# Probability transposes in chunks of 128 keys, and x2 moved to a multiple of 256 bytes, in a fused decoder layer

## The reference

```python
q = _split_heads(queries @ W_q + b_q)          # 16 heads of 32
k = _split_heads(keys @ W_k + b_k)
v = _split_heads(values @ W_v + b_v)
scores = jnp.einsum('bhqd,bhkd->bhqk', q, k) / jnp.sqrt(jnp.float32(d))
scores = jnp.where(mask == 0, jnp.float32(-1000000.0), scores)
attn = jax.nn.softmax(scores, axis=-1)
out = jnp.einsum('bhqk,bhkd->bhqd', attn, v)
...
return out @ W_o + b_o
...
x = _layernorm(x + _L0_ffn_ref(x, ...), axis=-1)   # x @ (kernel) + bias + (x @ a) @ b
```

## Time and profile before

| | |
|---|---|
| median of 3 runs | 945.8 us (941.78 to 947.99) |
| profiled execution | 944.69 us, its span 942.9 us |
| TensorE busy | 892.1 us, 4,348 matmuls |
| VectorE busy | 674.7 us |
| ScalarE, GpSimd busy | 377.3 us, 376.6 us |
| mean granted clock of TensorE | 0.981 |

### The profile page before, as it was taken

One profiled execution on the slowest core, in us unless ns is written; L12 is line 12 of the kernel. 1 busy time (PEld: TensorE's weight loads), 2 busy tenths in 40 slices (PEclk: granted clock), 3 DMA queues, 4 the chain that ended last, 5 costly groups with the idle time before them and its releaser, 6 DMA issues.

```text
span 942.9 us, 14474 instructions
## 1 busy us (share of the span) xinstructions
PE 892.1 (95%) x4348; PEld 739.6 (78%) x4348; DVE 674.7 (72%) x1132; ACT 377.3 (40%) x1403; POOL 376.6 (40%) x338
## 2 busy tenths in 40 slices
PE   5798999999999999999689999999999999999997
PEld 4683888888888888888568788888888888888775
DVE  3364566666665757667578878889788897888957
ACT  4161221202121111001596466665656656566611
POOL 2000464435354343333236534335343453434723
PEclk9897999999999999999799999999999999999999
DMA  6961811331404020204503040321303214031021
GB/s 183 284 201 57 173 39 53 82 91 44 134 11 122 22 67 23 67 38 140 175 16 109 21 135 15 93 71 26 133 13 91 71 28 131 13 91 23 14 78 46
DMA packets 85211, 76.03 MB, mean 81 GB/s; under 512 B 39143, under 2 KB 57831, under 8 KB 85167
## 3 DMA queue, kind: packets, MB, share of 16 engines
q1 hardware_dynamic: 85167, 75.49, 27.1%
HBM read 52.60 MB, written 22.87 MB: 80 GB/s over the span
## 4 chain that ended last, share of the span: by engine, by line
PE 42%; DVE 4%; ACT 2%; issue 2%; POOL 2%; POOLq 0%; DVEq 0%
PE shared_ps L114 31%; PE score_ps L114 4%; PE shared_ps L1185 4%; ACT probs L1391 1%; PE shared_ps L1148 1%; PE shared_ps L1218 1%; POOL probs L1540 1%; DVE score_ps L1697 1%; DVE xT_lo L1654 1%; DVE x_and_res L1743 0%; DVE pT_lo L1681 0%; DVE top_s L1702 0%; POOL x_and_res L1555 0%; DVE y L1721 0%; DVE w_o_lo L1864 0%
## 5 line engine op out<-in xcount | busy, mean ns | idle before, releaser
L1391 ACT ACTIVATE probs<-score_ps,top_s 128x77 f32<-128x77 f32 x512 | 159.1, 359 | 36.8 <-DVE top_s L1702 36.8
L1391 ACT ACTIVATION_READ_ACCUMULATOR probs<-score_ps,top_s 128x1 f32 x512 | 122.9, 240 | 0.0
L1540 POOL TENSOR_TENSOR probs<-probs,per_total 128x616 f32<-128x616 f32 x64 | 82.7, 1309 | 64.7 <-DVE per_total L1709 64.5
L1533 POOL TENSOR_TENSOR rstd<-ve,half_power 128x1 f32<-128x1 f32 x64 | 42.4, 662 | 156.7 <-DVE ve L1732 152.2
L1697 DVE COPY_PREDICATED score_ps<-hidden,masked 128x616 f32<-128x616 int32 x64 | 67.2, 1050 | 9.4 <-PE score_ps L114 9.3
L97 POOL TENSOR_TENSOR xT_lo<-x_tok,xT_hi 128x512 fp32r<-128x512 f32 x28 | 39.0, 1394 | 85.6 <-ACT xT_hi L93 85.6
L1398 ACT ACTIVATE pT_hi<-shared_ps 103x512 fp32r<-103x512 f32 (+1 forms) x96 | 54.9, 614 | 45.1 <-PE shared_ps L1185 44.6
L713 ACT ACTIVATE qT_hi<-vals 128x512 fp32r<-128x512 f32 x32 | 19.3, 628 | 119.2 <-POOL vals L760 103.9
L760 POOL TENSOR_TENSOR vals<-qs_prod 128x512 f32<-128x512 f32 x32 | 41.0, 1293 | 62.7 <-DVE qs_prod L846 62.7
L1681 DVE TENSOR_TENSOR pT_lo<-shared_ps,pT_hi 103x512 fp32r<-103x512 f32 (+1 forms) x96 | 64.5, 684 | 0.0
L706 ACT ACTIVATE v_sb<-v_ps 128x512 f32<-128x512 f32 x32 | 18.9, 594 | 106.9 <-PE v_ps L114 106.9
(11 more groups left out here) (210 smaller groups left out, 2642.5 us busy)
## 6 DMA issues: line engine op xcount, KB each, us to landing
x_tok<-in_x SPq DMA_DIRECT2D x32, 256.0 KB, 4.6
x_res<-in_x SPq DMA_DIRECT2D x8, 1024.0 KB, 7.3
x_between<-mix_x SPq DMA_DIRECT2D x32, 256.0 KB, 2.0
x<-x_between SPq DMA_DIRECT2D x8, 1024.0 KB, 5.6
x_tok<-x_between SPq DMA_DIRECT2D x8, 1024.0 KB, 5.7
out<-y_out SPq DMA_DIRECT2D x32, 256.0 KB, 2.0
wqkv_sb<-in_w_qkv SPq DMA_DIRECT2D x16, 192.0 KB, 5.0
keys_split<-w_q_hi SPq DMA_DIRECT2D x8, 154.0 KB, 5.0
```

The costliest lines, as they stand in the source:

```text
L1391: nc.scalar.activation(probs[:, t % 2, j * KEYS:(j + 1) * KEYS], score_ps[:, g, k * KEYS:(k + 1) * KEYS], ACT.Exp, bias=top[:, t % 2, j:j ...
L1533: nc.gpsimd.tensor_tensor(rstd[:, n:n + 1], ve[:, n:n + 1], half_power[:], ALU.pow).then_inc(rstd_ready, 1)
L1540: nc.gpsimd.tensor_tensor(p, p, per_total[:, t % 2, h * heads:(h + 1) * heads].unsqueeze(2) .to_broadcast([P, heads, KEYS]), ALU.mult).the ...
```

## The change

`KC` is gone. The probabilities of a tile are now cut per half (616 columns: two groups) into four chunks of 128 keys and a tail of 104 (`TAIL`). Bank uses: c = 0 has the four wide chunks of half 0, c = 1 those of half 1, c = 2 the two tails. The use with c = 0 waits for the first half of the normalization, c = 1 for the second. A group's 308 keys lie in three chunks, of which the middle one of a half is shared with the other group (`group_chunks`); its rows of the other group are zeros in `v_block`. The value pieces are cut anew and now differ between even and odd groups (`v_pieces`), so each DMA carries two groups and there are twelve pieces instead of six. `pT` has 10 chunks instead of 12, which moves the tiles behind it by 8,192 bytes. `x2T` starts at column 1,280 of its tile instead of 1,248.

```diff
--- before.py
+++ after.py
@@ -34,7 +34,10 @@
 GROUPS = D // P
 GH = XH // GROUPS
 GK = GH * KEYS
-KC = [(0, 103), (103, 103), (206, 102)]
+HALF = 2 * GK
+CHUNK = 128
+TAIL = HALF - 4 * CHUNK
+BANKS = [(0, 4, CHUNK), (4, 4, CHUNK), (8, 2, TAIL)]
 RANK = 16
 BLOCK = 32
 LINE = 32
@@ -98,13 +101,26 @@
                          ALU.subtract).then_inc(lo_ready, 1)
 
 
+def chunk_at(h, k):
+
+    return 4 * h + k if k < 4 else 8 + h
+
+
+def group_chunks(g):
+
+    h, first = g // 2, 2 * (g % 2)
+    return [(m, chunk_at(h, first + m), TAIL if first + m == 4 else CHUNK) for m in range(3)]
+
+
 def v_pieces():
 
-    for j in range(GH):
-        for c, (at, size) in enumerate(KC):
-            a, b = max(j * KEYS, at), min((j + 1) * KEYS, at + size)
-            if a < b:
-                yield j, c, a - at, a - j * KEYS, b - a
+    for odd in range(2):
+        for j in range(GH):
+            for m in range(3):
+                at = (2 * odd + m) * CHUNK - odd * GK
+                a, b = max(j * KEYS, at), min((j + 1) * KEYS, at + CHUNK, GK)
+                if a < b:
+                    yield odd, j, m, a - at, a - j * KEYS, b - a
 
 
 def split_matmuls(nc, out, pieces):
@@ -481,7 +497,7 @@
         flat = [t[:].rearrange("p c n -> p (c n)") for t in self.xT[1]]
         keys_end = GROUPS * GK
         self.k_block = [f[:, 0:keys_end].rearrange("p (g n) -> p g n", g=GROUPS) for f in flat]
-        at = (keys_end + LINE - 1) // LINE * LINE
+        at = (keys_end + 2 * LINE - 1) // (2 * LINE) * (2 * LINE)
         self.x2T = [f[:, at:at + NC * P].rearrange("p (c n) -> p c n", c=NC) for f in flat]
         self.mask, self.mask_loaded = sb("mask", [P, NT, KEYS], I32), sem("mask_loaded")
         sb("mask_to_line", [P, 8])
@@ -1006,10 +1022,10 @@
         sem = lambda n: ctx.enter_context(nc.semaphore(n))
         pair = lambda n, s: [sb(f"{n}_hi", s, F32R), sb(f"{n}_lo", s, F32R)]
         mask, mask_loaded = hand.mask, hand.mask_loaded
-        v_block = pair("v_block", [KC[0][1], len(KC), GROUPS, P])
+        v_block = pair("v_block", [P, 3, GROUPS, P])
         x1, res1, k_block, qT, oT, x2T = hand.x1, hand.x_first, hand.k_block, hand.qT, hand.xT[0], hand.x2T
         x2T_odd = [q[:, :, 0:P] for q in qT]
-        pT = pair("pT", [P, len(KC), GROUPS, S])
+        pT = pair("pT", [P, 10, S])
 
         x1T = oT
         w_o, w_ffn = ([sb(f"{w}_{k}", [P, NC, D], F32R) for k in ("hi", "lo")] for w in ("w_o", "w_ffn"))
@@ -1057,7 +1073,8 @@
 
         def turned_bank(s, t, c):
 
-            return shared_ps[s.bank(f"P{t}{c}")][0:KC[c][1], :].rearrange("p (g n) -> p g n", g=GROUPS)
+            _, chunks, size = BANKS[c]
+            return shared_ps[s.bank(f"P{t}{c}")][0:size, 0:chunks * P].rearrange("p (k n) -> p k n", k=chunks)
 
         @block.sync
         def _(sp):
@@ -1089,10 +1106,11 @@
 
                 wait_reuse(sp, oT_hi, i * NC)
                 for part in range(2):
-                    src = v_dram[part].rearrange("r (g j d) -> r g j d", g=GROUPS, j=GH)
-                    for j, c, row, key, n in v_pieces():
-                        sp.dma_start(v_block[part][row:row + n, c, :, j * XHD:(j + 1) * XHD].bitcast(F32),
-                                     src[bass.ds(i * KEYS + key, n)][:, :, j, :]).then_inc(v_loaded, 16)
+                    src = v_dram[part].rearrange("r (g b j d) -> r g b j d", b=2, j=GH, d=XHD)
+                    dst = v_block[part][:].rearrange("p m (g b) d -> p m g b d", b=2)
+                    for odd, j, m, row, key, n in v_pieces():
+                        sp.dma_start(dst[row:row + n, m, :, odd, j * XHD:(j + 1) * XHD].bitcast(F32),
+                                     src[bass.ds(i * KEYS + key, n)][:, :, odd, j, :]).then_inc(v_loaded, 16)
 
             def store(i, t):
                 sp.wait_ge(y_ready, nth(i, NT, t))
@@ -1176,14 +1194,15 @@
 
             def turn_probs(i, s, t, c):
 
-                if c == 0:
-                    pe.wait_ge(normed, nth(i, NT * 2, 2 * t + 1))
+                if c < 2:
+                    pe.wait_ge(normed, nth(i, NT * 2, 2 * t + c))
                 use = f"P{t}{c}"
                 wait_reuse(pe, freed, s.reusable(use))
-                at, size = KC[c]
-                for g in range(GROUPS):
-                    last = nc.tensor.transpose(shared_ps[s.bank(use)][0:size, g * P:(g + 1) * P],
-                                               probs[:, t % 2, g * GK + at:g * GK + at + size], ident[:])
+                _, chunks, size = BANKS[c]
+                for n in range(chunks):
+                    at = c * HALF + n * CHUNK if c < 2 else n * HALF + 4 * CHUNK
+                    last = nc.tensor.transpose(shared_ps[s.bank(use)][0:size, n * P:(n + 1) * P],
+                                               probs[:, t % 2, at:at + size], ident[:])
                 last.then_inc(turned, 1)
 
             def weigh_values(i, s, g):
@@ -1193,8 +1212,8 @@
                     pe.wait_ge(freed, s.emptied_before("P32"))
                     pe.wait_ge(turned_hi, nth(i, NT * 3, NT * 3 - 1))
                 wait_reuse(pe, freed, s.reusable(use))
-                pieces = [([v[0:size, c, g, :] for v in v_block], [p[0:size, c, g, :] for p in pT])
-                          for c, (_, size) in enumerate(KC)]
+                pieces = [([v[0:size, m, g, :] for v in v_block], [p[0:size, k, :] for p in pT])
+                          for m, k, size in group_chunks(g)]
                 split_matmuls(nc, shared_ps[s.bank(use)][:], pieces).then_inc(filled, 1)
 
             def project_o(i, s, t):
@@ -1394,8 +1413,8 @@
 
             def split_probs(i, s, t, c):
                 act.wait_ge(turned, nth(i, NT * 3, 3 * t + c))
-                size = KC[c][1]
-                nc.scalar.activation(pT[0][0:size, c, :, t * P:(t + 1) * P], turned_bank(s, t, c),
+                first, chunks, size = BANKS[c]
+                nc.scalar.activation(pT[0][0:size, first:first + chunks, t * P:(t + 1) * P], turned_bank(s, t, c),
                                      ACT.Copy).then_inc(turned_hi, 1)
 
             def split_o(i, s, g):
@@ -1675,11 +1694,10 @@
                           shared_ps[s.bank(f"T{t}")][:].rearrange("p (c n) -> p c n", c=NC))
 
             def split_probs(i, s, t, c):
-                size = KC[c][1]
+                first, chunks, size = BANKS[c]
                 dve.wait_ge(turned_hi, nth(i, NT * 3, 3 * t + c))
-                tok = slice(t * P, (t + 1) * P)
-                nc.vector.tensor_tensor(pT[1][0:size, c, :, tok], turned_bank(s, t, c),
-                                        pT[0][0:size, c, :, tok].bitcast(F32), ALU.subtract).then_inc(freed, 1)
+                hi, lo = (x[0:size, first:first + chunks, t * P:(t + 1) * P] for x in pT)
+                nc.vector.tensor_tensor(lo, turned_bank(s, t, c), hi.bitcast(F32), ALU.subtract).then_inc(freed, 1)
 
             def find_hidden(i):
                 dve.wait_ge(mask_loaded, nth(i, 1, 0) * 16)
```

## The result

The changed kernel takes 941.88 us (median of 5 runs, 940.63 to 942.98) against 945.8 us for the one before (941.78 to 949.45) beside it on the same chip: ratio 0.9947 with the interval [0.9926, 0.9969], some 4 to 5 us less. That lies within the forecast range, but is about half of the forecast gain of 8.2 us. The profiled execution took 941.81 us with a span of 939.4, 3.5 less than before's 942.9.

A forecast was written before the change was run, and what follows sets the result against it. The loop was taken as bound by the length of TensorE's list. Terms 3.9 + 0.8 + 0.9 + 1.3 + 1.6 = 8.5 us, less 0.3 for overlap, gave 945.8 - 8.2 = 937.6 us; range 933.5 to 942.3.

The forecast's parts named there:

- within 1%: Whole kernel: measured time differs from the kernel before by no more than 1%, given chance 0.75.
- signs named for a wrong prediction: Wide transposes at 120 ns or more, loop step above 58.4 or below 57.3 us, value or key loads among TensorE's releasers.
- A transpose costs 0.109 us whatever its columns: TensorE's list: each removed transpose saves 0.109 us, added columns cost 0; 7.0 us for the whole kernel.
- the case of the Trainium skill's rule on loaded columns: Rival on TensorE's transposes: 25 more columns cost 21 ns each, a tile saves 48 ns, total 941.6 us; chance 0.05.
- Three of four places in the loop keep the gain: Loop: three of four tiles keep their saved transposes, 0.65 us a step, 3.9 us over six steps.
- F0's loss: Before the loop's first feed-forward matmul: 0.22 us saved becomes a longer wait, from 0.5 to about 0.7 us.
- the value product behind it keeps its gain: Behind a step's last eviction: the eviction shortens by 0.27 us, TensorE comes 0.22 us earlier, so no gain is lost.
- Evictions, 0.13 us a step: Loop: third evictions fall to 0.41 us on VectorE, worth 0.13 us a step, 0.8 us in all, between 0 and 3.6.
- The closing step, −1.6 us: Closing step: six transposes fewer behind GpSimd's second half, 0.65 us at each of three stands; 1.6 us gained, between 0.9 and 2.6.
- The start, −1.3 us: Attention's start, batch 0 alone: eight transposes fewer and ScalarE's chain earlier; 1.3 us gained, between 0 and 2.
- x2's place, 0.9 us: Feed-forward groups: aligned x2 shortens weight loads from 192 to 188 ns; 0.03 us for each of 30 groups, 0.9 us.
- SyncE's queue at no cost: SyncE: 24 value load issues instead of 12 take 24.2 us a batch, but nobody waits for them; cost 0.

The follow-up runs named there:

- both_halves: Changed kernel, mask's constant still in SBUF, with each tile's first four transposes waiting for both halves of the normalization: 939.23 us, ratio 0.9923.
- before_strided_loads: Kernel before the change with each value load issued as two DMAs, one of groups 0 and 2, one of 1 and 3: 947.57 us, one run.
- x2_only: Kernel before the change with only the transposed x2 moved to a multiple of 256 bytes: 946.31 us, ratio 0.9993.
- before_mask_psum: Kernel before the change with the masked copy's constant in PSUM instead of SBUF: 943.24 us, ratio 0.997.

## Why the prediction was right, and where it was wrong

The range held and so did "within 1%", and none of the signs named for a wrong prediction came (109 ns, 58.02 us, no load among TensorE's releasers). But the total stayed in the range by luck: an unforeseen gain in step 1 made good a loss in the closing step. Against the steps of the sum:

- **A transpose costs 0.109 us whatever its columns: right.** 110 ns with 128 columns; a pair put back costs 0.21 to 0.24 us. With that the case of the Trainium skill's rule on loaded columns (TensorE: Matmul & The Clock Gate, LDWEIGHTS), 941.6 us, falls as a reason, though its number came close: no 21 ns per transpose is to be found.
- **Three of four places in the loop keep the gain: half wrong.** F0's loss came as forecast (wait 0.50 to 0.71 us). The other loss was not seen: "the value product behind it keeps its gain" failed. The last eviction stands behind `y_out`, which GpSimd's additions stretch to 1.02 us, and so the value product came late in the old kernel already (1.07 us behind the score where 0.84 is enough); the shorter eviction used itself up on that, and TensorE, 0.22 us earlier, waits 0.18 again. The transposes are worth 0.50 us a step rather than 0.65.
- **Evictions, 0.13 us a step: too small.** 0.416 us was forecast to the hundredth, partly by luck, as the middle between two estimates of 0.34 and 0.47; but their effect is 0.4 us a step in a TensorE list of equal length. I had bounded it by 0.6 and taken the low side because TensorE's idle time looked small; short delays under overlapping matmuls do not show there, as the 0.18 us before the first value product.
- Together, without the collisions of the masked copy, the loop gives 1.02 us a step where the sum has 0.65 + 0.13 + 0.12 = 0.90: near, because the transposes bring 0.15 less and the evictions 0.3 more. **Collisions took 0.31 of it** (57.71 against 58.02), and this is the first failed step: the terms were added as if VectorE's other instructions kept their lengths.
- **The closing step, −1.6 us: the step of the sum that failed outright.** It became 2.1 us longer. Two masked copies fell behind GpSimd instructions, 1.0 us each; without such copies it is still 0.35 us longer than the old one, not 1.6 shorter. The six transposes at each stand were priced on TensorE's list in a stage where they do not count: two put back per tile cost nothing (48.26 us against 48.36), and GpSimd's halves released earlier bring nothing (48.36 with, 48.31 without). That VectorE, busy 34.61 of 38 us, sets the end there is argued from TensorE's waits for it, and not shown.
- **The start, −1.3 us: not shown.** 42.5 us against 42.0, in a part that varies by 4 us between kernels. At a like clock the traces point both ways: 40.7 us (both_halves, 0.87) against 42.0 (before, 0.88) and 42.5 (after, 0.76) against 43.4 and 44.5 (before_strided_loads and x2_only, 0.76 and 0.77), but with the constant in PSUM 43.6 against 42.9 (both 0.80).
- **x2's place, 0.9 us: right in size (0.7 to 1.0), wrong in the reason given.**
- **Not in the sum: step 1, −4.4 us,** of which 0.65 is a loop step's gain and the rest a copy of 3.75 us with a clock loss behind it that the old kernel had.
- **SyncE's queue at no cost: right.**

The balance of step 1, loop and closing step: the sum had 6 × 0.9 + 1.6 = 7.0 us of gain there. Without the collisions of the masked copy the six steps bring 0.5 more (5.1 + 0.8 instead of 5.4) and the closing step 1.95 less (0.35 lost instead of 1.6 gained). Collisions, each taken against the same kernel with the constant in PSUM, move step 1 by +3.5, the loop by −1.9 (1.5 lost in the new kernel, 0.35 won by them in the old one) and the closing step by −1.7 (2.1 in the new, 0.4 in the old). That makes 7.0 + 0.5 − 1.95 + 3.5 − 1.9 − 1.7 = 5.45; the traces show 4.36 + 3.24 − 2.07 = 5.53. (The two agree by construction, up to rounding: the balance sorts the differences and proves none of them.) What the spans show less than that, 2.0 us, lies in the parts ahead, at the start and at the end.

What stays open: whether the longer `y_out` is why the closing step without the copies' collisions is 0.35 us longer in the new kernel; whether the start gained anything; why one copy stood through three GpSimd instructions; and why the matmuls of the feed-forward groups stand closer with x2 at its new place.

## What to carry to other kernels

Before pricing an edit by mean durations, look at the same instruction's shortest and longest times; where they differ by a factor of two, ask what ran beside the long ones, because an edit that shifts the engines by a few tenths of a microsecond can move a collision into or out of the path. VectorE instructions that read twice from SBUF, or copy from SBUF to SBUF, should not stand on the path beside GpSimd work: moving one operand to PSUM was worth here about as much as the change itself, and starting the GpSimd work later another 1.3 us. And a gain priced on TensorE's list counts only in stages where that list sets the end.

## What the runs showed of the hardware

- A VectorE copy under a mask with both inputs in SBUF takes 0.80 us alone, 1.8 to 1.9 us when a GpSimd instruction began 0.06 to 0.13 us earlier, and 3.75 us across three GpSimd instructions in a row; with one input in PSUM always 0.80 (five kernels). A scaling from SBUF to SBUF (128 x 512) goes from 0.54 to 1.02 us, in the closing step to 1.12. GpSimd's instruction is the one that gets longer when it began later (1.27 to 1.83 us), though once also when it had begun 0.38 us earlier (887.41 in before_mask_psum, 1.99 us).
- The copy of 3.75 us waited not only for the GpSimd instruction that ran when it started but also for two that began after it (508.65). That is the exception: the copies at 878.59 in the changed kernel and the first ones of every loop step got in as soon as the running GpSimd instruction ended, and the next one, right behind it, became the long one (1.77 to 1.85 us).
- Issues of DMAs of 128-byte pieces follow each other on SyncE every 1.01 us with four neighbouring groups, every 0.47 us with two, and every 1.0 us with two that are not neighbours.
- After a wait of 2.32 us TensorE's clock was down to half from 522.2 to 525.6 us in the kernel before, so that wait cost some 1.5 us more than its own length (an estimate: eight matmuls started 0.42 us apart instead of 0.23). Waits of 1.7 us in the closing step of after had no such stretch behind them.
